# Decoder stack of six stages on one core: the first expert stage adds its results by token in DRAM, with six shared groups ahead of its list

## The reference, cut to what matters

```python
h2 = rmsnorm(X, norm2_w).reshape(B * S, d)
probs = jax.nn.softmax(h2 @ router_w)
topw, topi = jax.lax.top_k(probs, 2)
topw = jax.nn.softmax(topw, axis=-1)
combine = jnp.sum(jax.nn.one_hot(topi, 8) * topw[..., None], axis=1)
shared = swiglu(h2, sh_gate, sh_up, sh_down)
gate, up = einsum('td,edf->etf', h2, e_gate), einsum('td,edf->etf', h2, e_up)
eout = einsum('etf,efd->etd', silu(gate) * up, e_down)
return X + shared + einsum('etd,te->td', eout, combine)
```

## Time and profile before

| | us |
|---|---|
| median of 3 runs | 3291.21 (3287.84 to 3295.37) |
| the profiled execution | 3287.47 |
| its span, first to last instruction | 3285.3 |
| TensorE busy (matmul) | 2739.6 |
| VectorE, ScalarE, GpSimd busy | 1904.1, 1520.3, 1452.9 |
| stage d, features to the next stage's start | 1397 to 2066 |
| stage f, last row of the profile | 2953 to 3285 |

### The profile page before, as it was taken

The page is one execution under the profiler, slowest core; times in us unless marked ns, Lnnn a source line. Parts: engine busy times, 40 slices in busy tenths (PEclk is TensorE's granted clock), DMA queues, the critical chain, the costliest instruction groups (busy, mean ns, idle before and its releaser), DMA issues.

```text
span 3285.3 us, 49090 instructions
## 1 busy us (share of the span) xinstructions
PE 2739.6 (83%) x16588; PEld 1861.5 (57%) x16588; DVE 1904.1 (58%) x3444; ACT 1520.3 (46%) x2639; POOL 1452.9 (44%) x1633
## 2 busy tenths in 40 slices
PE   6888888857887888786999998799788888749997
PEld 2333333325564566533888875697555555537776
DVE  3888888866887688751222224402789998851111
ACT  4566665535775666410222210443666666522222
POOL 3666676654444577525000006300455555532333
PEclk8999999999998999988999999799999999869999
DMA  9600000000012000022566652100000000007675
GB/s 325 218 1 0 1 1 0 1 0 30 20 66 76 1 1 1 1 71 91 182 219 210 210 164 81 54 1 1 7 28 33 29 28 28 21 34 218 189 198 131
DMA packets 131956, 243.97 MB, mean 74 GB/s; under 512 B 15184, under 2 KB 103376, under 8 KB 121040
## 3 DMA queue, kind: packets, MB, share of 16 engines
q1 hardware_dynamic: 112320, 207.36, 19.4%
q0 software_dynamic: 19440, 34.10, 4.3%
HBM read 154.90 MB, written 87.43 MB: 74 GB/s over the span
## 4 chain that ended last, share of the span: by engine, by line
PE 24%; POOL 9%; issue 8%; DMA 7%; DVE 6%; ACT 2%; POOLq 1%; another core or an unknown queue 1%; SPq 0%; DVEq 0%; ACTq 0%
PE PS L2305 8%; DMA out<-f_y,f_token 6%; PE PS L1892 4%; PE PS L2261 4%; POOL e_hs L1451 2%; POOL rows_by_expert L2192 2%; POOL out L2621 1%; POOL e_qs L1454 1%; POOL rows_in_place L872 1%; PE PS L1306 1%; DVE e_mx L1354 1%; PE PS L1883 1%; PE PS L1249 1%; POOLq L2661 1%
## 5 line engine op out<-in xcount | busy, mean ns | idle before, releaser
L572 POOL TENSOR_TENSOR u_in<-dtx,b_rep 128x512 f32<-128x512 f32 x256 | 325.0, 1292 | 201.2 <-ACT b_rep L553 200.0
L588 DVE TENSOR_TENSOR_SCAN state<-PS,u_in 128x512 f32<-128x512 f32 x256 | 312.2, 1220 | 59.0 <-POOL u_in L572 34.8
L545 PE MATMUL PS<-scaled,ident 128*128 128x512 f32 x512 | 295.9, 662 | 28.2 <-DVE scaled L582 28.1
L2326 ACT ACTIVATE d_act_b<-PS 128x256 f32<-128x256 f32 (+2 forms) x192 | 76.1, 399 | 486.9 <-PE PS L2305 398.5
L1451 POOL TENSOR_TENSOR e_hs<-e_pr 128x512 f32<-128x512 f32 x128 | 162.7, 1271 | 231.0 <-ACT e_pr L1418 227.6
L2305 PE MATMUL PS<-d_unit_T,d_w 128*128 128x256 f32 (+1 forms) x1280 | 261.8, 358 | 1.0 <-ACT d_unit_T L2315 1.0
L2338 DVE TENSOR_TENSOR d_hid<-d_act_b,PS 128x256 f32<-128x256 f32 (+2 forms) x192 | 84.2, 440 | 295.9 <-ACT d_act_b L2326 276.5
L561 ACT ACTIVATE PS<-dt,decay_rate 128x508 f32<-128x508 f32 x256 | 173.5, 687 | 138.1 <-DVE state L588 136.4
L2305 PEld LDWEIGHTS PS<-d_unit_T,d_w 128*128 128x128 f32 x1280 | 222.0, 191 | 26.3 <-issue 1.4
L2621 POOL DMA_INDIRECT out<-f_y,f_token x71 | 110.2, 1553 | 218.8 <-DVE f_y L2612 160.8
L582 DVE TENSOR_TENSOR scaled<-state,PS 128x512 f32<-128x512 f32 x256 | 169.5, 665 | 55.5 <-PE PS L526 43.9
(11 more groups left out here) (451 smaller groups left out, 6477.0 us busy)
## 6 DMA issues: line engine op xcount, KB each, us to landing
d_w<-in_d_w SPq DMA_DIRECT2D x42, 1024.0 KB, 5.1
f_w<-in_f_w SPq DMA_DIRECT2D x40, 1024.0 KB, 5.1
rows_in_place<-blank SPq DMA_DIRECT2D x136, 272.0 KB, 5.0
d_w<-in_d_w SPq DMA_DIRECT2D x42, 512.0 KB, 4.0
rows_by_expert<-zeros SPq DMA_DIRECT2D x36, 256.0 KB, 2.6
f_unit_rows<-rows_in_place SPq DMA_DIRECT2D x31, 272.0 KB, 5.3
d_unit_rows<-rows_by_expert SPq DMA_DIRECT2D x31, 256.0 KB, 4.2
out_by_expert<-d_y_rows SPq DMA_DIRECT2D x31, 256.0 KB, 4.2
```

Of the source, the lines that this page charges most:

```text
L545: nc.tensor.matmul(YB[:, c], ident[:], scaled[:, (KD * n + c) % RC], start=False, stop=n == NS - 1).then_inc(m_y, 1)
L572: nc.gpsimd.tensor_tensor(u_in[:, k % RU], dtx[:, p, c], b_rep[:, n % RB], ALU.mult).then_inc(m_u, 1)
L588: nc.vector.tensor_tensor_scan(state[:, k % 2], DECAY[:, k % RD], u_in[:, k % RU], 0.0, ALU.mult, ALU.add).then_inc(m_h, 1)
```

## The change

The rows of the list in stage d now carry the shares of all eight experts and the token number, as those of stage f do: H is made wider (H_wide, with ROW columns), the router writes the shares into it, and GpSimd the token numbers, which TensorE and VectorE make at the stage's start. The scatter reads H itself, so nothing is staged; before every third scatter GpSimd waits for a further quarter of TensorE (`full`). Six shared groups (SHN = NG - 2) stand ahead of the list and two behind it. For each unit VectorE notes the share and the token of each row (`note_vector`), scales on evacuation into one of four `y_rows` buffers, and GpSimd adds the tile by token to `out_by_token` in DRAM, which holds zeros at first; it waits for each unit's landing. When all have landed, SyncE loads the sums of a group (512 KB each, four buffers), and VectorE adds them to X in one operation for each group: six in the last shared group, two behind it. In stage f, `y` and `token` get four buffers.

```diff
-    rows_by_expert = nc.dram_tensor("rows_by_expert", (PLACES * UR, D), F32, kind="Internal").ap()
-    out_by_expert = nc.dram_tensor("out_by_expert", ((2 * FULL + SINGLE) * 128, D), F32, kind="Internal").ap()
     ROW = D + 2 * E
+    rows_by_expert = nc.dram_tensor("rows_by_expert", (PLACES * UR, ROW), F32, kind="Internal").ap()
+    out_by_token = nc.dram_tensor("out_by_token", (NG * GT, D), F32, kind="Internal").ap()
...
-    def experts(tag, turn, src, gated, rows_by_expert, out_by_expert, listed, result=None):
+    def experts(tag, turn, src, src_wide, rows_by_expert, out_by_token, listed):
         E = 8
-        SHN = NG // 2 if gated else 0
+        SHN = NG - 2
+        OUT = 4
...
+            link(V.tensor_tensor(lg[:], best[:, 0], by_e(top[:, 0]), ALU.mult))
+            link(V.tensor_tensor(tmp[:], best[:, 1], by_e(top[:, 1]), ALU.mult))
+            dve.wait_ge(marked, 2)
+            link(V.tensor_tensor(src_wide.rearrange("p g k d -> p (g k) d")[:, :, D:D + E], lg[:], tmp[:], ALU.add))
...
+            link(V.tensor_scalar(names[:], order, -1.0, float(E), ALU.mult, ALU.add))
+            link(V.tensor_tensor(mine[:], expert_f[:].unsqueeze(2).broadcast_to([128, UNITS, E]),
+                                 names[:].unsqueeze(1).broadcast_to([128, UNITS, E]), ALU.is_equal))
...
-        def stage_group(dve, turn, p):
-
-            g = 2 * turn + p
-            after(dve, in_list[p], 16 * 2 * GS * turn)
-            nc.vector.tensor_copy(staged_rows[:, p], rows_full[:, g])
-            nc.vector.tensor_copy(slot_now[:, p], slot[:, g]).then_inc(staged, 1)
...
         def to_list_pool(pl):
-            pl.wait_ge(listed, 16 * PLACES)
-
-            def group(turn, p):
-                g = 2 * turn + p
-                after(pl, marked, g)
-                pl.wait_ge(staged, g + 1)
-                nc.gpsimd.tensor_tensor(mark[:], eps[:, 0:1], eps[:, 0:1], ALU.add).then_inc(marked, 1)
+            pl.wait_ge(listed, 16 * (PLACES + NG * GT // UR))
+            pl.wait_ge(marked, 2)
+            pl.wait_ge(placed, 1)
+            for g in range(NG):
                 for k in range(GS):
                     for j in range(2):
+                        at = 2 * (g * GS + k) + j
+                        if at and at % 3 == 0:
+                            pl.wait_ge(full, at // 3)
                         nc.gpsimd.indirect_dma_start(
-                            rows_by_expert, bass.IndirectOffsetOnAxis(slot_now[:, p, k, j:j + 1], 0),
-                            staged_rows[:, p, k], None).then_inc(in_list[p], 16)
-
...
-        def collect_group(dve, turn, p):
-            g = 2 * turn + p
-            if SHN:
-                dve.wait_ge(taken, 2 * (g + 2 + (UNITS if g >= SHN else 0)))
-            dve.wait_ge(combined, g + 2)
-            nc.vector.tensor_copy(share_now[:, p], share[:, g]).then_inc(share_set, 1)
-            dve.wait_ge(share_set, g + 1)
-            dve.wait_ge(got[p], 16 * 2 * GS * (turn + 1))
...
+                            rows_by_expert, bass.IndirectOffsetOnAxis(slot[:, g, k, j:j + 1], 0),
+                            src_wide[:, g, k], None).then_inc(in_list[g % 2], 16)
+
+        def to_tokens_pool(pl):
+            done = 0
+            for j in range(UNITS):
+                pl.wait_ge(taken, 2 * (j + SHN) + 4)
+                for k in range(tiles_at[j]):
+                    nc.gpsimd.indirect_dma_start(
+                        out_by_token, bass.IndirectOffsetOnAxis(token[:, j % OUT, k:k + 1], 0), y_rows[:, j % OUT, k], None,
+                        bounds_check=NG * GT - 1, oob_is_err=False, compute_op=ALU.add).then_inc(added, 16)
+                done += tiles_at[j]
+                pl.wait_ge(added, 16 * done)
+                pl.sem_inc(scattered, 1)
+
+        def note_vector(dve, j, jp, kind, q=0):
+            n = tiles_of[kind]
+                dve.wait_ge(row_in[jp], 8 * (j - jp) + 16)
+            nc.vector.tensor_tensor(mine_rows[:, jp, 0:n], unit_rows[:, jp, 0:n, D:D + E],
+                                    mine[:, j].unsqueeze(1).broadcast_to([128, n, E]), ALU.mult).then_inc(weighed, 1)
+            dve.wait_ge(scattered, j + 1)
+            nc.vector.tensor_copy(token[:, q, 0:n], unit_rows[:, jp, 0:n, D + E]).then_inc(noted, 1)
+            dve.wait_ge(weighed, 2 * j + 1)
+            nc.vector.tensor_reduce(share_rows[:, jp, 0:n], mine_rows[:, jp, 0:n], AX.X, ALU.add).then_inc(weighed, 1)
+
+        def collect_group(dve, g):
+            dve.wait_ge(taken, 2 * (g + 2 + (UNITS if g >= SHN else 0)))
+            dve.wait_ge(got[g % GOT], 16 * (g // GOT + 1))
+            nc.vector.tensor_tensor(X[:, g], X[:, g], y_got[:, g % GOT], ALU.add).then_inc(combined, 1)
...
-                if kind == "shared" and again is None and (f == 1 or f == 3 and ahead):
-                    stage_group(dve, u + f // 2, 1 - f // 2)
...
+                if f == 3 and ahead in tiles_of:
+                    note_vector(dve, at + 1, 1 - p, ahead, (q + 1) % OUT if kind != "shared" else 0)
+                if again == NG - SHN - 1 and f > 0:
+                    for g in (2 * f - 2, 2 * f - 1):
+                        collect_group(dve, g)
...
 
             if kind != "shared":
-                turns = 16 * (at // 2) if isinstance(at, int) else 8 * (at - p)
-                dve.wait_ge(y_out[p], turns + 16)
+                dve.wait_ge(scattered, at + 1)
+                dve.wait_ge(weighed, 2 * at + 2)
...
-                    step = nc.vector.tensor_copy(y_rows[:, p, h:h + 1], o)
+                    step = nc.vector.tensor_scalar(y_rows[:, q, h], o[:, 0], share_rows[:, p, h:h + 1], None, ALU.mult)
...
-            SHR = lambda g, gp, r=0: ("shared", g, gp, r)
-            LST = lambda j, jp, kind="list": (kind, j, jp, ring_of(jp))
+            SHR = lambda g, gp, r=0: ("shared", g, gp, r, 0)
+            LST = lambda j, q, kind="list": (kind, j, q % 2, ring_of(q % 2), q)
...
         def load_rows(sp, j, jp, at, tiles):
             after(sp, turned, j - 1)
+            after(sp, weighed, 2 * j - 3)
+            after(sp, noted, j - 1)
             sp.dma_start(unit_rows[:, jp, 0:tiles], list_rows[:, bass.ds(at, tiles)]).then_inc(row_in[jp], 16)
...
-        def store_out(sp, j, jp, at, tiles):
-            sp.wait_ge(taken, 2 * (j + SHN) + 4)
-            sp.dma_start(out_rows[:, bass.ds(at, tiles)], y_rows[:, jp, 0:tiles]).then_inc(y_out[jp], 16)
...
-            sp.wait_ge(placed, 1)
+            sp.dma_start(w[:, 0, 0:UPS], ins[f"{tag}_w"][E][:, 0:UPS]).then_inc(w_gu[0], 16)
+            sp.dma_start(w[:, 0, UPS:], ins[f"{tag}_w"][E][:, UPS:]).then_inc(w_dn[0], 16)
+            sp.wait_ge(placed, 2)
...
+            sp.wait_ge(scattered, UNITS + OUT)
+            for g in range(NG):
+                after(sp, combined, g - GOT + 1)
+                sp.dma_start(y_got[:, g % GOT], out_rows[:, g]).then_inc(got[g % GOT], 16)
...
             pe.wait_ge(loaded, 48)
+            pe.wait_ge(counted, 1)
+            nc.tensor.matmul(PS[:, 6, 0:1], before_me, ones[:, 0:1], start=True, stop=True).then_inc(counted, 1)
...
+            nc.vector.memset(ones[:], 1.0).then_inc(counted, 1)
...
         def pool(pl):
             for u, half in enumerate(half_of(NG)):
                 step = nc.gpsimd.memset(unit_no[:, u:u + 1], float(half))
             step.then_inc(numbered, 1)
-            rows["pool"](pl)
+            marks_pool(pl)
             to_list_pool(pl)
-            collect_pool(pl)
+            to_tokens_pool(pl)
...
-        RING = 3
+        RING, OUT = 3, 4
...
-                after(dve, added, 16 * late(u - RING + 1))
-                nc.vector.tensor_copy(token[:, r, 0:n], rows[:, r, 0:n, D + E]).then_inc(sent_to, 1)
+                after(dve, added, 16 * late(u - OUT + 1))
+                nc.vector.tensor_copy(token[:, u % OUT, 0:n], rows[:, r, 0:n, D + E]).then_inc(sent_to, 1)
...
-                after(dve, added, 16 * late(u - 1))
+                after(dve, added, 16 * late(u - OUT + 1))
                 for k in range(n):
                     dve.wait_ge(down, upto[u] + k + 1)
-                    nc.vector.tensor_scalar(y[:, u % 2, k], DB(k), share[:, k:k + 1], None, ALU.mult).then_inc(mixed, 1)
...
-    H = h_mem.take("H", [128, NG, GS, D])
+    H_wide = h_mem.take("H", [128, NG, GS, ROW])
+    H = H_wide[:, :, :, 0:D]
...
-    zeros = z_mem.take("zeros", [128, UR // 128, D])
+    zeros = z_mem.take("zeros", [128, UR // 128, ROW])
...
-                sp.wait_ge(zeroed, 1)
+                sp.wait_ge(zeroed, 2)
                 with sp.Fori(0, PLACES) as u:
                     sp.dma_start(rows_by_expert.rearrange("(u r p) d -> p u r d", p=128, r=UR // 128)[:, u], zeros[:]).then_inc(listed, 16)
+                with sp.Fori(0, NG * GT // UR) as u:
+                    sp.dma_start(out_by_token.rearrange("(u r p) d -> p u r d", p=128, r=UR // 128)[:, u], zeros[:, :, 0:D]).then_inc(listed, 16)
...
-                nc.gpsimd.memset(zeros[:], 0.0).then_inc(zeroed, 1)
```

(2 more changed lines are left out.)

258 lines of the change are left out of this document (91 added, 167 removed).

## The result

Over seven runs each, the changed kernel takes **3265.12 us** in the median (3260.88 to 3278.37) and the kernel before 3288.19 (3280.98 to 3295.37): ratio 0.9937, 95% interval [0.9915, 0.9958]. That is 23 us less where 51.5 were forecast. The sign and the range held, the size did not.

A forecast was written before the change was run, and what follows sets the result against it. TensorE was taken to bound stage d's list, with idle time around it to remove. Gains of 54.8 us, less 5.3 given back, plus 2 in stage f, made 51.5: 3291.2 to about 3240 us, range 3222 to 3276.

The forecast's parts named there:

- Second list: four output buffers: Stage f: GpSimd's chain of landings stays, earlier weights may shorten the last two landings; 2 us gained, bounds -6 and +6.
- My sign for stage f: What would show the forecast right: the second list still takes about 300 us, with GpSimd let go by landings.
- the four steps of stage d: First expert stage: shared groups ahead 20.1, start of the list 13.4, last groups 12.4, tail 8.9; together 54.8 us gained.
- Cold clock: Stage d: matmuls slowed after TensorE's idle times regain full speed; 2.9 + 1.8, 1.9 + 1.3 and 1.7 us gained.
- Stalls that survive: Shared groups ahead of the list: 2.0 us given back for stalls of ScalarE that remain despite spaced scatters.
- the router: Start of stage d: extra VectorE operations lengthen TensorE's first wait of 4.72 us by 0.8, bounds 0 and 2.
- Whatever the mechanism is, it comes with long unbroken runs of indirect DMAs: First shared groups: ScalarE's stalls go with long scatter runs, so spacing the scatters removes them; 20.1 us with the cold clock.
- rival 1: Shared groups of stage d: stalls stay at each of five boundaries, 33.5 us instead of 2.0, total 3271; chance 0.20.
- 2 (weights late): List of stage d: weight loads come late beside scatter-adds, 15 us instead of 2, total 3253; chance 0.08.
- 3 (the chain bounds the list): List of stage d: GpSimd's scatter-add landings become the bound, 489 instead of 402 us at landings of 10, total 3327; chance 0.05.
- 5 (sums late): Last groups of stage d: sums load late, VectorE holds the last group by 10 us, total 3250; chance 0.06.
- Rival 4: Stage f: the buffers free the second list to TensorE's pace, 268 from 303 us, 35 more gained, total 3205; chance 0.06.

The follow-up runs named there:

- e1: The changed kernel with the second list put back to two output buffers and three for row numbers: 3236.8 us, ratio 0.9829.
- e2: The kernel before with only the second list's edit, four output buffers and four for row numbers: 3321.2 us, ratio 1.0093.
- e13: The kernel of e3 with GpSimd waiting for a quarter at every twelfth scatter instead of every third: 3225.4 us, ratio 0.9810, stage d 626.6 us.
- e11: The kernel of e5 run again on another chip, instruction for instruction the same: 3274.6 us, ratio 0.9941, stage d 670.5 us.
- e12: The kernel of e3 run again in a later set: 3214.3 us, ratio 0.9765, stage d 613.5 us.
- e5: The kernel of e3 without GpSimd's waits between the scatters of stage d, all 64 in one run: 3209.6 us, ratio 0.9841.
- e8: The kernel before with H laid out in rows of 1088 bytes, nothing else changed: 3263.8 us, ratio 1.0011, stage d 641.5 us.
- e10: The changed kernel run again, unchanged, in a later set: 3264.5 us, ratio 0.9920.
- e9: The kernel before run again, unchanged, in a later set: 3286.8 us in one run, stage d 673.0 us.
- e3: The changed kernel with eight buffers for the second list's row numbers beside four for outputs: 3214.7 us, ratio 0.9766.
- e14: The kernel of e5 once more, as control for e13 on the same chip: 3272.9 us in one run, stage d 670.3 us.
- e7: The changed kernel with only the first three units of stage f loading weights, a probe with other results: 3192.2 us, ratio 0.9789.

## Why the prediction was wrong, and where it was right

**Failed: "Second list: four output buffers ... -2 (bounds -6 and +6, as weights and scatters meet otherwise)".** Measured: +27.5 in the profiles, +28 in e1 and e2. I had read that GpSimd is let go by a landing, that its wait stays, and that the buffers therefore give nothing; that was right. I then priced the meeting of weights and scatters at 6 us, from the spread of the landings in one arrangement. But the change makes one arrangement the rule: in each turn from the 12th to the 34th the weights go out 1.24 to 1.64 us behind the unit's first scatter-add, where before they went out now ahead of it and now behind. And a landing in GpSimd's chain counts 40 times: 5.96 us in place of 5.33 in the mean is 24.5 of the 27.6 us of the chain. And I read the waits in the order of GpSimd's code, not of VectorE's: the edit moved VectorE's wait from the evacuation to the copy of the row numbers, whose semaphore gates SyncE's queue. Who is queued behind a wait that the change adds was asked for stage d and not here. My sign for stage f, "GpSimd let go by landings", held; "about 300 us" did not.

The Trainium skill ("DMA: Bandwidth & Descriptors", Queues, rings and completion order) has each of the 16 engines go round its queues packet by packet; by that rule a transfer in flight delays another. The traces of stage f fit that, though they show no single packet's turn: landings of 3.9 us without the weights, 6.3 with them. I had held this rule against the weights in stage d, where it brought nothing, and not against stage f, where a landing is the bound.

**Held: the four steps of stage d**, on chips with the stalls. Idle time of TensorE: 44.9 us gone, 45.2 forecast (15.4 + 10.2 + 10.7 + 8.9). Cold clock: 11.1 of busy time gone, 9.6 forecast. The tail is 3.16 for 4.4. The list starts 171.3 us into the stage for 170.7, and lasts 399.9 for 400 to 404. (The time of the 64th scatter was added up wrongly, 1452.5 + 12.3 + 4 x 20.7 being 1547.6 and not 1549; nothing rests on the difference.)

**Too dear: what I had given back.** Stalls that survive 0 of 2.0; row numbers 0 of 0.5, the stretch ahead of the first group being 40.84 us where 40.9 stood before; weights late in the list 0 of 2.0 (TensorE idles 1.05 in 399.9); only the router is dearer, its wait 6.0 for 4.72, 1.3 of 0.8. So 1.3 us were given back in place of 5.3, 4.0 of the 6.5 us by which stage d beat its sum; the cold clock brought 1.5 more than forecast, and the idle time, without the router's 1.3, another 1.0.

**Right for another reason, or only in places.** "Whatever the mechanism is, it comes with long unbroken runs of indirect DMAs": e13 and e11 show that the waits grow with the run. The Trainium skill ("Runtime: NRT & Kernel Launch", Instruction fetch mechanics) has another cause of a stall, a taken branch out of the fetched window. By rival 1 spacing the scatters would then be useless; e11 and e12, one chip and 57 us apart by that spacing, speak against it as the whole cause. A fetch that the scatters themselves hold up isn't ruled out by this, but nothing here bears it out: from 1500 to 1547 us, in the stall of e11, the trace has 1681 DMA packets of queue q0 and 325 of q1, and none of an instruction queue. Where e5 to e8 ran there are no such waits, ungated (e5) or in the code of before (e8). The idle time of the last groups is partly of that kind too (before, ScalarE has "remote" waits of 27.6 us there and VectorE of 26.0): e8 has 2.1 us of it in one wait, the profile of before had 12.16. There the kernel before loses 641.5 - 613.4 = 28.1 us to the new stage d, at the start of the list and in the tail, and 27.5 of that would be lost in stage f; the change itself was not run on it, so that it gains next to nothing there is an estimate.

**Not forecast: 8 us ahead of stage d.** The same kernel gives the recurrence 748.9 and 742.3 us (after, e10), 741.6 and 746.3 (before, e9), 748.8 and 754.1 (e3, e12), and 741.4, 748.9 and 751.7 (e5, e11, e14). Over all profiles the mean is 744.6 for the four with the old stage d and 747.4 for the fourteen with the new one, within that spread. The lengths go with TensorE's clock at the start of each of eight groups; after the change the matmuls of line 536, and in the repeat of the same kernel (e10):

```profile
L536 PE MATMUL PS<-xconv,skip_w x32: 592/1057/1222, 52.4 to 655.8; 128*128 128x512 f32 x32
```

```profile
L536 PE MATMUL PS<-xconv,skip_w x32: 592/697/1219, 52.0 to 651.0; 128*128 128x512 f32 x32
```

(The three numbers are ns, least, median and most.) The same matmul takes 1057 ns in the median in one and 697 in the other, with recurrences of 748.9 and 742.3 us. At the third group's start (from 223 us) its four matmuls run at a granted clock of 0.50 after the change and 1.00 in e10, the lower and the full level. The median is 697 ns in the six profiles with a recurrence under 743 us, and 924 to 1061 in the twelve of 745 us and more. Most of the 8 us is chance between executions; what sets it is open, and a few us from the change are not excluded.

**The rivals.** 1 (stalls at each boundary), 2 (weights late), 3 (the chain bounds the list) and 5 (sums late) did not come: the loads of the sums start at 1983.23 us, six after the list's end at 1977.0, and are there when VectorE needs them at 2001.66. Rival 4 (buffers free the second list) came to nothing in the change, and to 24 of its 35 us in e3 (first to last scatter-add 278.7 us for 302.7): buffers do free it, through shorter landings rather than fewer waits.

## What to carry to other kernels

Before a buffer is made deeper, list the waits of every engine in the order of its own program, with the ring depth of each: the shallowest ring decides where the engine stands, among equally deep ones the first in the program (here, with 4 and 4, the copy of the row numbers), and what is queued behind that place moves with it. If a bound is a chain through DMA landings, ask what else goes out in the same microsecond, and multiply by the number of turns. And keep long work of one engine's DMAs in short runs: that cost nothing on a chip that did not need it (stage d 613.3 in e7, 613.4 ungated in e5) and was worth 57 us where it did.

## What the runs showed of the hardware

- The same program stalls in one set of runs and not in another, each on its own chip: 65.64 us of ScalarE during a run of 64 indirect DMAs in e11, none in e5, with 670.5 and 613.4 us for the stage. The kernel before took 3259.9 us on the chip without them and 3287 to 3294 on the others. Ratios from different sets can't be put beside each other: in stage d gated and ungated scatters differ by 57 us on one chip (e12, e11) and by nothing on another (e7, e5).
- An indirect scatter-add of 128 rows of 1 KB in stage f lands in 3.9 us in the median with no weight load beside it (e7), in 4.6 with the load ahead of it (e3), and in 6.3 with the load issued between a unit's two scatter-adds (after). Loads alone don't fix the number: in the list of stage d, with 1.5 MB of weights for each unit, it is 3.9 in the median and 8.6 at most.
- TensorE's granted clock at the starts of the recurrence's groups differs between executions of one kernel (0.50 and 1.00 in the same four matmuls, after and e10), with recurrences up to 10 us apart (741.4 and 751.7 in e5 and e14, on two chips).
